# Two-layer block kernel on one core: four of 32 feed-forward gates are moved to later tiles of the attention loop, and the splitting of the weights starts two tiles sooner

## The reference

```
xn = layernorm(x)
q, k = rope(xn @ wq), rope(xn @ wk);  v = xn @ wv
attn = softmax(causal(q @ k.T / 128)) @ v @ wo
h = silu((xn @ w1.T) * s1) * ((xn @ w2.T) * s2)      # 512 hidden: "the gates"
h = gelu((h @ h1.T) * sh1);  h = gelu((h @ h2.T) * sh2)
x = x + attn + (h @ w3.T) * s3
```

## Time and profile before

| what | value |
|---|---|
| median of 3 runs | 276.53 us (276.32 to 276.6) |
| the profiled execution | 277.21 us, its span 275.1 us |
| TensorE busy | 258.8 us, 94% of the span |
| VectorE, ScalarE, GpSimd busy | 216.1, 191.4, 100.8 us |
| mean granted TensorE clock | 0.992 |

### The profile page before, as it was taken

The page is one execution under the profiler, slowest core; times in us unless marked ns, Lnnn a source line. Parts: engine busy times, 40 slices in busy tenths (PEclk is TensorE's granted clock), DMA queues, the critical chain, the costliest instruction groups (busy, mean ns, idle before and its releaser), DMA issues.

```text
span 275.1 us, 5406 instructions
## 1 busy us (share of the span) xinstructions
PE 258.8 (94%) x1794; PEld 169.7 (62%) x1798; DVE 216.1 (79%) x733; ACT 191.4 (70%) x467; POOL 100.8 (37%) x130
## 2 busy tenths in 40 slices
PE   6899999999978889999999999999999999999993
PEld 2379845456653634767777777778687444444483
DVE  6977579999997589889999979778850797666684
ACT  1487489886655379688755799999661897777730
POOL 9314000000000067898875579889772000000000
PEclk9999999999999799999999999999999999999999
DMA  7700000000000191400000000000000000000005
GB/s 198 212 14 2 2 0 4 0 1 0 2 2 0 23 397 44 152 2 4 0 2 0 0 2 0 4 1 0 0 2 2 0 0 0 4 1 0 0 10 147
DMA packets 8287, 8.51 MB, mean 31 GB/s; under 512 B 1729, under 2 KB 7362, under 8 KB 7746
## 3 DMA queue, kind: packets, MB, share of 16 engines
q1 hardware_dynamic: 7826, 7.84, 9.0%
q10 hardware_dynamic: 432, 0.30, 0.4%
HBM read 7.09 MB, written 1.05 MB: 30 GB/s over the span
## 4 chain that ended last, share of the span: by engine, by line
PE 58%; DVE 29%; ACT 7%; issue 3%; DMA 2%; SPq 0%; DVEq 0%; ACTq 0%
PE PS L862 10%; PE PS L861 10%; PE PS L834 9%; PE PS L811 8%; PE PS L824 4%; PE PS L495 3%; DVE arena L1592 3%; PE PS L514 3%; DVE arena L1579 2%; DVE arena L1624 2%; DVE arena L1829 2%; DVE mxb L1844 2%; DVE arena L1615 2%; DMA x<-L_attn_x 2%; PE PS L784 2%
## 5 line engine op out<-in xcount | busy, mean ns | idle before, releaser
L861 PE MATMUL PS<-arena 128*128 128x512 f16 x128 | 48.5, 379 | 0.0
L862 PE MATMUL PS<-arena 128*128 128x512 f16 x128 | 48.5, 379 | 0.0
L1902 DVE TENSOR_TENSOR arena<-arena 128x512 f32<-128x512 f32 x32 | 22.2, 693 | 13.6 <-ACT arena L1292 13.6
L811 PE MATMUL PS<-arena 128*128 128x512 f32 (+3 forms) x80 | 31.9, 530 | 0.0
L1291 ACT ACTIVATE arena<-PS,arena 128x512 f32<-128x512 f32 x32 | 22.7, 710 | 9.6 <-PE PS L862 9.6
L1352 POOL CAST arena<-arena 128x512 f16<-128x512 f32 x2 | 1.3, 645 | 73.6 <-ACT x L1157 73.6
L1344 POOL TENSOR_TENSOR arena<-arena 128x256 f32<-128x256 f32 x32 | 21.5, 672 | 14.5 <-DVE arena L1836 12.6
L1265 ACT ACTIVATE arena<-PS,lnt 128x512 f32<-128x512 f32 (+3 forms) x40 | 24.9, 632 | 1.6 <-DVE lnt L1851 1.4
L1345 POOL TENSOR_TENSOR arena<-arena,small 128x256 f16<-128x256 f32 (+1 forms) x36 | 23.8, 660 | 2.8
L1292 ACT ACTIVATE arena<-PS,arena 128x512 f16<-128x512 f32 x32 | 22.6, 707 | 0.0
L1844 DVE TENSOR_REDUCE mxb<-PS 128x1 f32<-128x512 f32 (+3 forms) x40 | 22.2, 602 | 0.3 <-PE PS L813 0.2
(11 more groups left out here) (282 smaller groups left out, 649.8 us busy)
## 6 DMA issues: line engine op xcount, KB each, us to landing
arena<-h_T SPq DMA_DIRECT2D x2, 1024.0 KB, 5.7
x<-L_attn_x SPq DMA_DIRECT2D x4, 256.0 KB, 4.7
arena<-cos SPq DMA_DIRECT2D x1, 1024.0 KB, 4.8
arena<-sin SPq DMA_DIRECT2D x1, 1024.0 KB, 7.0
out<-arena SPq DMA_DIRECT2D x4, 256.0 KB, 2.3
arena<-w_T SPq DMA_DIRECT2D x3, 256.0 KB, 3.0
con<-shape_constants ACTq DMA_DIRECT2D x1, 192.0 KB, 3.4
w1e<-L_ffn_W SPq DMA_DIRECT2D x1, 128.0 KB
```

The source lines that it names most:

```text
L811: i = mm(PS[:, k, 0:cnt * P], qT1[:, t * P:(t + 1) * P], kT1[:, c * P:(c + cnt) * P], start=True, stop=not last)
L861: mm(bank(b), wH[:, k, m * P:(m + 1) * P], sH[:, k, cols], start=(k == 0), stop=False)
L862: i = mm(bank(b), wL[:, k, m * P:(m + 1) * P], sL[:, k, cols], start=False, stop=(k == HT4 - 1))
L1902: v.tensor_tensor(RP[m], FP[m], high, ALU.subtract).then_inc(rest_ready, 1)
```

## The change

The late gates of tiles 6 to 9 are taken out of these tiles: LATE_GATES has now one gate in tiles 10 and 11, and turn 16 gets an early and a late one. The 32 gates keep their order, so all behind the eleventh (u = 10) move down by up to four places. GATES_AT[12] becomes 22 in place of 24. WT_TILE goes from 9 to 7, so the weights are split in turns 7 to 12 on ScalarE, 8 to 13 on GpSimd and 9 to 14 on VectorE. GpSimd's loop runs over turn 16 as well, for the low parts of the last two gates.

```diff
-WT_TILE = 9
+WT_TILE = 7
...
-        EARLY_GATES, LATE_GATES = (0, 0, *(2,) * (FULL - 2), *(1,) * (NT - FULL), 0), (*(0,) * 6, 1, 1, 1, 1, 0, 0, *(1,) * (NT - FULL), 0)
+        EARLY_GATES, LATE_GATES = (0, 0, *(2,) * (FULL - 2), *(1,) * (NT + 1 - FULL)), (*(0,) * (FULL - 2), 1, 1, *(1,) * (NT + 1 - FULL))
...
-            for t in range(NT):
+            for t in range(NT + 1):
                 for u in (*GATE_EARLY[t], *GATE_LATE[t]):
                     gate_parts(u)
                 for i in weights_with(t - 1):
                     weights(i)
```

## The result

The changed kernel took 281.35 us in the median of 4 runs (279.61 to 282.47) against 276.56 before (4 runs, 276.32 to 277.54): 1.0143 times as long, with a 95% interval of 1.0107 to 1.0179. The quotient of the two medians by itself is 1.0173, so the kernel is slower by 4.0 us going by the ratio and by 4.8 going by the medians. Six runs more beside its variants gave 1.0149 (1.0103 to 1.0194). The forecast was 279.6 in a range of 276.8 to 281.0; the median lies 0.35 above the upper end, while the ratio, taken on the 276.53 of the forecast, gives 280.5, inside it.

What follows compares the result with a forecast made beforehand. TensorE, busy 258.8 of 275.1 us, was taken as the bound, with other queues close behind. +1.3 to 1.4 at turn 16's start, +3.1 with turn 16, on 276.53 gave 279.6 us; range 276.8 to 281.0.

Steps and rivals of the forecast that it cites:

- Part 1: Tiles 6 to 8: TensorE's three stalls at late gates go, with the pipe's refills; 1.9 us of gain.
- Part 2: Tiles 9 to 11: weights sooner crowd ScalarE, so its copies come late; 0.5, 0.3 and 0.25 us.
- Part 3: Start of tile 12: scores wait for tile 11's late gate in bank 3; TensorE stands about 2.3 us.
- Part 4: Tile 13: GpSimd's packed queue finishes array 7 at 178.5, delaying VectorE's maxima; TensorE 1.4 us late.
- a sign that I had named: Turns 11 to 13: VectorE at L1882 would wait for GpSimd's L1380 at some turn.
- I had charged 0.4: Turns 9 to 12: 0.4 us a gate for VectorE copies slowed beside a never idle GpSimd.
- the 192 that I had given: From tile 8 on: GpSimd would have no idle from 146 to about 192 us.
- Part 5: Last turns: two gates in turn 16 cost 0.9, TensorE stands 0.7 plus 0.17 refill; turn's sum +1.7 us.
- rival 4: Tile 12: the 2.3 us stall drops the clock, TensorE loses 1.7 more; 281.3 us, chance 0.08.
- rival 1: Tiles 12 and 13: waits at their low end, S12' = 167.3, no loss in 13; 278.1 us, chance 0.22.
- rival 2: Tile 12: VectorE sets the pace, stall under 0.2, the stalls' gain reaches the end; 275.5 us, chance 0.11.
- rival 3: Whole kernel: a wash, half of each loss against 1.9 gain, turn 16 hidden; 276.2 to 277.0 us, chance 0.09.

Runs made afterwards that it cites:

- gates_only: The changed kernel's gate moves alone, weights from tile 9 as in the kernel before; 277.59 us, 1.0019 against the kernel before.
- light_act: fill12 with ScalarE leaving out the low fp16 part of the nine later weight arrays, one-column copies instead; 280.42 us, 1.0116 against the kernel before.
- bank6_w9: gates_only with tile 11's late gate in bank 6, so tile 12's scores wait for bank 3 alone; 277.27 us, 0.9998 against the kernel before.
- fill12: The changed kernel with eight unused matmuls ahead of TensorE's wait at tile 12; 280.9 us, 1.0148 against the kernel before.
- w7_only: The kernel before with WT_TILE 7 in place of 9 alone, gates where they were; 281.71 us, 1.0177 against the kernel before.
- late11_to_9: The changed kernel with the late gate of tile 11 back in tile 9, weights still from tile 7; 280.67 us, 1.0126 against the kernel before.
- late9_w9: Against the kernel before: weights from tile 9, late gates of tiles 6 to 8 moved, to tile 10 and turn 16; 276.22 us, 0.9982.
- experiment 5: Four kernels with other gate placements and weights from tile 9, against the kernel before; medians 276.22 to 277.27 us, ratios 0.9974 to 0.9998.

## Why the prediction was nearly right, and where it fell short

**Part 1 (stalls go): right.** No idle at L784 in tiles 6 to 8; tile 9 at 31.55, forecast 31.5. The gain of 1.9 is in gates_only at tile 9 as well: 34.79 - 31.54 = 3.25, of which three gates are 1.35.

**Part 2 (ScalarE): right in size.** Tile 10 at 38.19 and tile 11 at 45.57, each 0.1 to 0.2 behind the forecast, and light_act shows the 0.55 and 0.3 as ScalarE's.

**Part 3 (tile 12): right, cause and size.** A stall of 2.43 us, forecast 2.3, released by the late gate. With the bank changed (bank6_w9) the stall of 1.61 us of gates_only is gone, and tile 12 starts 1.01 us sooner.

**Part 4 (GpSimd): right in cause, wrong in the way it costs.** Array 7 was done at 178.30, which is 179.0 on before's scale; forecast 178.5. But neither in the changed kernel nor in fill12 does any row show VectorE idle at L1882 for GpSimd, which was a sign that I had named; w7_only and late11_to_9 alone show that wait. What made tile 13 longer in fill12 is the copy ahead of the reductions, 1.08 us in place of 0.29, for which I had charged 0.4. And the cost isn't in tile 13 alone: in w7_only it is 3.5 us already at tile 12. Since tile 12 was late for the late gate anyhow, my sum came near all the same: 73.66 at tile 14 with the clock up (fill12), forecast 73.2. That this came out so close with a wait put where a held-up copy was is in part luck. GpSimd's break of 0.23 at 179.84 came sooner than the 192 that I had given. The Trainium skill ("SBUF — State Buffer", the section "Who interferes with whom") says that VectorE in a two-port mode and GpSimd exclude each other, and that the second to come stands still for the whole instruction of the first. The trace agrees in the copies that last to the end of GpSimd's operation (1.11 and 1.32 us in light_act).

**Part 5 (last turns): right, the stall 0.2 too large.** Idle of 0.49 before the first gate of turn 16, under the 0.6 to 0.8 that I had given, and 0.66 with the refill, forecast 0.87. Gelu began later, and from tile 15 to the end the kernel took 1.68 us more than before, forecast 1.7, so hardly anything was lost by it.

**The step that failed is the clock, which I left out of the sum and made rival 4.** I gave it 0.08, on the ground of "one pause, with work without a break on both sides", and named a granted clock of 1.00 in tile 12 as a sign. One pause was enough in both profiles, where it was 0.63 (from 168 to 172.6) and 0.57 (from 168 to 172). Its price, 1.7, was of the right size: the scores took 4.56 us (168.04 to 172.60) against 2.90 in fill12 (168.22 to 171.12). Of the whole it is 1.0 to 1.5, since in fill12 tile 13 pays part of it for GpSimd (9.47 us, against 8.91 and 8.69 in the two others). On the scale from tile 1 this is the miss: forecast 166.0, with filler 166.26, without 167.29 and 167.77.

Forecast and rival together make 281.3, and the measured median is 281.35. So close a match is luck: single executions run from 279.6 to 282.5, and the filler, which kept the clock up in its profile, has a median of 280.9, 1.3 above my 279.6. Why it lies so much higher than its profiled loop (0.3 over the forecast) was not followed; the stretch ahead of tile 1 differs by up to 1.9 us between profiles.

The Trainium skill ("TensorE: Matmul & The Clock Gate", the section "HAM oscillation — how this bites in real kernels") describes waits between bursts that drop the clock again and again; in this case one such wait of 2.4 us dropped it once. I weighed the absence of a drop in the loop before against it, though the loop before had no pause of that length in it: its longest was 0.6.

Rivals 1, 2 and 3 are out: tile 12 began at 56.5, where rival 1 had 55.1 (its 167.3), the stall there was 2.43 where rival 2 needs it under 0.2, and rival 3's 276.2 to 277.0 supposes half of each loss, where the kernel is 4 us and more slower.

## What to carry to other kernels

Follow each in-order queue through the turns with the durations of the trace, the one with the lowest share of busy time too. GpSimd was busy for 37% of the span, but the change packed 35 us of its work together, and there VectorE's copies beside it grew from 0.29 to over 1 us. When a unit of work is moved, look for waits that name a count of such units: moving one gate behind the update of x turned a wait of some 0.15 us into one of 2.4, because of the bank that it sat in. A new pause of TensorE as long as this one can have a second price after it, at the clock, and then belongs into the sum and not among the rivals.

## What the runs showed of the hardware

The granted clock fell to 0.63 in the scores that followed a pause of TensorE of 2.43 us (and of 2.44 in the second profile), and stayed at 1.00 after 1.61 us in gates_only's profile and after pauses of 0.3 to 1.3 us elsewhere in the loop. Filler matmuls in the pause, which left 0.5 us of it idle, kept it at 1.00. The level in the slow part was 0.50 in both profiles.

VectorE's copy of 128x256 from f32 to f16 took 0.29 us with GpSimd standing (before, at 176.95) and up to 1.37 beside a GpSimd operation of 1.26 that had begun just ahead of it (late9_w9, from 178.94).

Code that is the same in all kernels, ahead of tile 1, took 111.22 to 113.13 us in the profiles, which is as much as the differences that experiment 5 looks for. The starts of tiles counted from tile 1 agree within 0.03 us between kernels where their code is the same, and so tell apart what the medians of 12 runs do not.
